# Perceiver layer on one core: key/value projection and cross attention in one loop over chunks, and the general path moved to the end

## The reference

```python
x = x + xattn(layernorm(x), ctx, ctx, ctx, ctx, ...)   # 16 heads of 32, 512 queries, keys: ctx twice
x = x + attn(layernorm(x), ...)                        # sequence axis of length 1: softmax is 1
x = x + ffn(layernorm(x), ...)                         # 8 experts, top 2, gelu, 512 -> 2048 -> 512
# xattn:
k = (jnp.einsum('bke,fe->bkf', k_full, wk) + bk).reshape(B, Lkv, H, D)
v = (jnp.einsum('bke,fe->bkf', v_full, wv) + bv).reshape(B, Lkv, H, D)
scores = jnp.einsum('bqhd,bkhd->bhqk', q, k) * scale
attn = jax.nn.softmax(scores, axis=-1)
ctx = jnp.einsum('bhqk,bkhd->bqhd', attn, v).reshape(B, Lq, E)
```

## Time and profile before

| | us |
|---|---|
| median of 3 runs (lowest, highest) | 1449.85 (1448.89, 1450.54) |
| the profiled execution | 1445.7 |
| its span, first to last instruction | 1443.9 |
| to the end of `project_queries` | 29.9 |
| projection of keys and values | 358.7 |
| end of that block, flag, skipped `find_maxima` | 8.0 |
| attention | 590.8 |
| cross output / self attention / routing | 27.1 / 35.4 / 29.1 |
| experts and end | 364.9 |

### The profile page before, as it was taken

How to read it: one execution, slowest core, us unless ns; L and a number is a source line. 1 busy time by engine, 2 the same in 40 slices (tenths; PEclk the granted TensorE clock), 3 DMA queues, 4 the chain that set the end, 5 groups by cost and what they waited for, 6 DMA issues and landing times. The chain is left out here.

```text
span 1443.9 us, 20528 instructions
## 1 busy us (share of the span) xinstructions
PE 1370.8 (95%) x7608; PEld 847.3 (59%) x7608; DVE 950.6 (66%) x819; ACT 772.9 (54%) x841; POOL 73.6 (5%) x71
## 2 busy tenths in 40 slices
PE   5999999999799999999999999998769999999995
PEld 4888888888643333333333333333557787887873
DVE  7444444444288888888888888887653566766662
ACT  4122221221088888888888888884222445555541
POOL 2000000000030000000000000000102010111110
PEclk9999999999999999999999999999955999999998
DMA  6854555556396555555555555520804666676641
GB/s 207 266 175 179 193 199 184 174 193 196 136 260 131 112 112 112 112 109 114 116 116 116 116 116 116 114 61 1 306 5 147 220 216 211 232 243 206 239 132 40
DMA packets 140900, 225.07 MB, mean 156 GB/s; under 512 B 8776, under 2 KB 41672, under 8 KB 140848
## 3 DMA queue, kind: packets, MB, share of 16 engines
q1 hardware_dynamic: 137520, 217.12, 51.7%
q0 software_dynamic: 3344, 7.47, 2.1%
HBM read 162.61 MB, written 59.85 MB: 154 GB/s over the span
## 5 line engine op out<-in xcount | busy, mean ns | idle before, releaser
L663 ACT ACTIVATE at_p<-at_s 128x1024 f32<-128x1024 f32 x512 | 496.9, 1023 | 90.7 <-PE at_s L616 90.6
L683 DVE TENSOR_TENSOR p_sum<-p_sum,at_p 128x2048 f32 (+1 forms) x208 | 476.7, 2292 | 58.1 <-ACT at_p L663 51.1
L616 PEld LDWEIGHTS at_s<-q_stack,at_k 97*128 97x128 f32 x1024 | 172.7, 189 | 248.5 <-ACT at_p L663 162.0
L616 PE MATMUL at_s<-q_stack,at_k 97*128 (+1 forms) x1024 | 311.4, 424 | 7.5 <-PEq L444 6.7
L629 PE MATMUL at_o<-at_p,at_v 128*32 128x512 f32 x2048 | 272.7, 605 | 0.1
L143 ACT ACTIVATE sc_c_hi<-sc_c 128x2048 fp32r<-128x2048 f32 x16 | 30.7, 1920 | 151.0 <-PE sc_vp L388 137.6
L413 ACT ACTIVATE sc_k_hi<-sc_kp,sc_bk 128x512 fp32r<-128x512 f32 x64 | 44.2, 691 | 125.4 <-PE sc_kp L381 125.4
L345 DVE SCALAR_TENSOR_TENSOR sc_k_lo<-sc_kp,sc_bk,sc_k_hi 128x512 fp32r<-128x512 f32 x64 | 47.8, 749 | 89.0 <-ACT sc_k_hi L413 89.0
L353 DVE TENSOR_TENSOR sc_v<-sc_vp,sc_bv 128x512 f32<-128x512 f32 x64 | 44.1, 689 | 88.8 <-PE sc_vp L388 88.8
L1268 ACT ACTIVATE se_h<-se_hp,se_b_cur 128x160 f32<-128x160 f32 x128 | 43.4, 391 | 105.4 <-PE se_hp L1203 105.4
L1255 ACT ACTIVATE se_wi_hi<-ei_wi 128x2048 fp32r<-128x2048 f32 x32 | 61.2, 1913 | 69.4 <-DVE se_b_cur L1314 69.1
(11 more groups left out here) (225 smaller groups left out, 1534.4 us busy)
## 6 DMA issues: line engine op xcount, KB each, us to landing
at_k<-k_hi_scratch SPq DMA_DIRECT2D x128, 256.0 KB, 4.8
ei_wi<-w_in SPq DMA_DIRECT2D x32, 1024.0 KB, 7.4
ei_wo<-w_out SPq DMA_DIRECT2D x32, 1024.0 KB, 5.5
sc_c<-ctx_t SPq DMA_DIRECT2D x16, 1024.0 KB, 7.9
k_hi_scratch<-sc_k_hi SPq DMA_DIRECT2D x16, 1024.0 KB, 4.0
k_lo_scratch<-sc_k_lo SPq DMA_DIRECT2D x16, 1024.0 KB, 6.1
at_k<-k_lo_scratch SPq DMA_DIRECT2D x64, 256.0 KB, 4.2
at_v<-v_scratch SPq DMA_DIRECT2D x64, 256.0 KB, 4.9
```

The lines of the kernel that those rows point to most:

```text
L616: last = nc.tensor.matmul(s[r][:, a * NQ:(a + 1) * NQ], k[c][:, j, t * P:(t + 1) * P], q_stack[:, bass.ds(it // PER_GROUP * (HG * NQ) + j ...
L663: nc.scalar.activation(p[t % PR][:, pair * 2 * NQ:(pair + 1) * 2 * NQ], s[u % SR][:, :], ACT.Exp, scale=SCALE).then_inc(p_ready[t % PR], 1)
L683: nc.vector.tensor_tensor(sums, sums, p[t % PR][:, :], ALU.add).then_inc(p_summed[t % PR], 1)
```

## The change

`stream_context`, the first `find_maxima` and `attend` are replaced by one block `attend_stream`. It projects the eight pieces of chunk 0 first; then, for every chunk, 16 steps (4 head groups by 4 key tiles) are worked in eight doubles of two steps, and one of the eight pieces of the next chunk is projected in each double (the last key group of a chunk in its own first double). Keys `k_hi`, `k_lo` (one buffer) and values (two) stay in SBUF; nothing goes to DRAM. Scores are no longer one product over 97 stacked rows: for each part the four heads of a group are four products over their own 32 rows, at row positions 0, 32, 64, 96, into four PSUM banks. All probabilities are summed by VectorE; `BY_PE` and `total_acc` go. Bank `o` now ends after 4 tiles. The value bias moves to the output: values carry no bias, and `cross_output` adds bv x Wo to the output bias. No bound is computed beforehand; `cross_output` looks at the logarithms of the totals (`good`), `route` joins that with the length flag to `again`. `any_path` holds the whole layer once more, in its general form (with maxima, any expert length), as eight stages in one block behind the output; each engine loads `again` once and guards each stage with it. Other edits: the late weights are loaded when the last projection is done; `turn_tokens` does its four large transposes and then its four small ones.

```diff
+def attend_stream(nc, ctx, c_dram, o_acc, p_sum, a, late, late_dram):
...
+    SR, PR = 3, 4
+    STEPS = NG * KT
+    DOUBLES = STEPS // 2
+    PAIRS = NCH // 2
+    k_hi, k_lo = (sb(f"k_{n}", [P, NG, CH], F32R) for n in ("hi", "lo"))
+    v = [sb(f"v{b}", [P, KT, E]) for b in range(2)]
+    p = [sb(f"p{r}", [P, HG * NQ]) for r in range(PR)]
+    s = [ctx.enter_context(nc.psum_tensor(f"as_s{r}", [P, 2 * NQ], F32)) for r in range(SR)]
+    o = ctx.enter_context(nc.psum_tensor("as_o", [P, NQ], F32))
+    proj = ctx.enter_context(nc.psum_tensor("as_proj", [P, CH], F32))
...
+    OUTPUTS = [("v", 0), ("k", 0), ("v", 1), ("k", 1), ("v", 2), ("k", 2), ("v", 3), ("k", 3)]
+    first_banks = [proj[:, :], o[:, :]] + [s[r][:, h * NQ:(h + 1) * NQ] for r in range(SR) for h in range(2)]
...
+            with sp.Fori(1, NCH) as m:
+                sp.wait_ge(c_lo_ready, ET * m)
+                sp.dma_start(c[:, :, :], c_dram.rearrange("(t p) n -> p t n", p=P)[:, :, bass.ds(m * CH, CH)]).then_inc(c_loaded, 16)
+            sp.wait_ge(k_done, NG * NCH)
+            for to, src in zip(late, late_dram):
...
+                for part, (lhs, rhs) in enumerate(products):
+                    for d in range(ET):
+                        if kind == "v":
+                            left, right = lhs[b][:, d, i * P:(i + 1) * P], rhs[:, d, E:2 * E]
+                        else:
+                            left, right = lhs[:, d, i * P:(i + 1) * P], rhs[b][:, d, :]
+                        last = nc.tensor.matmul(bank, left, right, start=(part == 0 and d == 0),
+                                                stop=(part == 2 and d == ET - 1))
+                last.then_inc(v_done if kind == "v" else k_done, 1)
+            def scores(i, b, step):
+                n, g, t = 2 * i + b, step // KT, step % KT
+                if t == 0:
+                    pe.wait_ge(k_lo_ready, NG * n + g + 1)
+                if isinstance(n, int) and n == 0 and step < 2:
+                    pe.wait_ge(k_lo_ready, NG - 1 + step)
+                    pe.wait_ge(v_ready, KT - 1 + step)
+                for pair in range(2):
+                    u = (b * STEPS + step) * 2 + pair
+                    if u >= SR:
+                        w = u - SR
+                        pe.wait_ge(p_ready[w // 2 % PR], exped(2 * i, w // 2, w % 2))
+                    else:
+                        w = s_last[u % SR]
+                        wait_reuse(pe, p_ready[w // 2 % PR], exped(2 * i - 2, w // 2, w % 2))
+                for part, (keys, queries) in enumerate(((k_hi, q_hi), (k_lo, q_hi), (k_hi, q_lo))):
+                    for j in range(HG):
+                        rows, r = slice(j * D, (j + 1) * D), ((b * STEPS + step) * 2 + j // 2) % SR
+                        last = nc.tensor.matmul(s[r][:, j % 2 * NQ:(j % 2 + 1) * NQ], keys[rows, g, t * P:(t + 1) * P],
+                                                queries[rows, g, :], start=(part == 0), stop=(part == 2))
+                        if part == 2 and j % 2 == 1:
+                            last.then_inc(s_ready[r], 1)
+            def outputs(n, b, step):
+                g, t = step // KT, step % KT
+                if t == 0:
+                    wait_reuse(pe, o_added, NG * n + g)
...
+                pe.wait_ge(p_ready[step % PR], exped(n, step, 1))
+                for j in range(HG):
+                    feats = slice(g * P + j * D, g * P + (j + 1) * D)
+                    last = nc.tensor.matmul(o[j * D:(j + 1) * D, :], v[b][:, t, feats], p[step % PR][:, j * NQ:(j + 1) * NQ],
+                                            start=(t == 0), stop=(t == KT - 1))
+                last.then_inc(p_used[step % PR], 1)
...
+                        scores(i, b, 2 * j)
+                        if j == 0 and not begins:
+                            project(n, b, *OUTPUTS[-1], proj[:, :], False)
+                        elif j > 0 and not ends:
+                            project(n + 1, 1 - b, *OUTPUTS[j - 1], proj[:, :], False)
+                        scores(i, b, 2 * j + 1)
+                        for step in (2 * j - 2, 2 * j - 1):
+                            if step >= 0:
+                                outputs(n, b, step)
+                            elif not begins:
+                                outputs(n - 1, 1 - b, step + STEPS)
+            for (kind, i), bank in zip(OUTPUTS, first_banks):
+                project(0, 0, kind, i, bank, True)
+            rolled(pe, PAIRS, pair)
...
+            def keep(m, b, kind, i, bank):
+                if kind == "v":
+                    if i == 0:
+                        wait_reuse(act, o_done, NG * (m - 1))
+                    act.wait_ge(v_done, KT * m + i + 1)
+                    nc.scalar.activation(v[b][:, i, :], bank, ACT.Copy).then_inc(v_ready, 1)
+                else:
+                    act.wait_ge(k_done, NG * m + i + 1)
+                    nc.scalar.activation(k_hi[:, i, :], bank, ACT.Identity, bias=bk[:, i:i + 1]).then_inc(k_hi_ready, 1)
...
+                        exps(i, b, 2 * j)
+                        if j == 0 and not begins:
+                            keep(n, b, *OUTPUTS[-1], proj[:, :])
+                        elif j > 0 and not ends:
+                            keep(n + 1, 1 - b, *OUTPUTS[j - 1], proj[:, :])
+                        if 2 <= j < 2 + ET and not last:
+                            split(n + 2, b, j - 2)
+                        exps(i, b, 2 * j + 1)
...
+            for (kind, i), bank in zip(OUTPUTS, first_banks):
+                keep(0, 0, kind, i, bank)
+            for d in range(ET):
+                split(1, 1, d)
...
+            def add_outputs(n, g):
+                dve.wait_ge(o_done, NG * n + g + 1)
+                if isinstance(n, int) and n == 0:
+                    nc.vector.tensor_copy(o_acc[:, g, :], o[:, :]).then_inc(o_added, 1)
+                else:
+                    nc.vector.tensor_tensor(o_acc[:, g, :], o_acc[:, g, :], o[:, :], ALU.add).then_inc(o_added, 1)
...
+                        add_probabilities(n, 2 * j)
+                        if j == 0 and not begins:
+                            keep_low(n, OUTPUTS[-1][1], proj[:, :])
+                        elif j > 0 and not ends and OUTPUTS[j - 1][0] == "k":
+                            keep_low(n + 1, OUTPUTS[j - 1][1], proj[:, :])
+                        if j % 2 == 1 and j > 1:
+                            add_outputs(n, (j - 3) // 2)
+                        elif j == 1 and not begins:
+                            add_outputs(n - 1, NG - 1)
+                        if 2 <= j < 2 + ET and not last:
+                            split(n + 2, b, j - 2)
+                        add_probabilities(n, 2 * j + 1)
...
@@ cross_output @@
+            pe.wait_ge(widened, NG + 1)
+            for g in range(NG):
+                last = nc.tensor.matmul(out[0][:, :], bv_wide[:, g, :], wo[:, g, :], start=(g == 0), stop=(g == NG - 1))
+            last.then_inc(bias_done, 1)
+            pe.wait_ge(bias_added, 1)
...
+            dve.wait_ge(bias_done, 1)
+            nc.vector.tensor_tensor(bo_all[:, :], bo[:, :], out[0][:, :], ALU.add).then_inc(bias_added, 1)
@@ route @@
+                last = nc.tensor.matmul(ranks[:, (QT + 1) * NX:(QT + 1) * NX + 1], every[:, :], good[:, :], start=True, stop=True)
@@ class General @@
+    def guarded(self, eng, name):
+        if name not in self.flags:
+            self.flags[name] = eng.value_load(self.flag[:, :], min_val=0, max_val=1)
+        with eng.If(self.flags[name] > 0):
...
+            self.meet(eng, 2 * self.stage - 1)
+            if name in self.programs:
+                self.programs[name](eng)
+            self.meet(eng, 2 * self.stage)
```

More of the change, by code:

```diff
@@ L21 @@
+import math
 from contextlib import ExitStack
@@ L319, in _ @@
-            for j in range(HG):
-                rows = slice(j * D, (j + 1) * D)
-                for part, src in enumerate((q_hi, q_hi, q_lo)):
-                    dst = q_stack[part * D:(part + 1) * D, :].bitcast(F32).rearrange("d (g j q) -> d g j q", j=HG, q=NQ)
-                    sp.dma_start(dst[:, :, j, :], src[rows, :, :].bitcast(F32)).then_inc(a.stacked, 16)
-            rolled(sp, PAIRS, pair)
-            sp.wait_ge(a.stacked, 16 * 3 * HG)
-            sp.wait_ge(stored[0], STORES * PAIRS)
@@ L699, in cross_output @@
-def cross_output(nc, ctx, wo, bo, o_acc, p_sum, total_acc, x_sb):
-    sb = lambda n, s, d=F32: ctx.enter_context(nc.sbuf_tensor(n, s, d))
-    sem = lambda n: ctx.enter_context(nc.semaphore(n))
+                    begins, ends = isinstance(n, int) and n == 0, last and b == 1
+                    for j in range(DOUBLES):
+                        add_probabilities(n, 2 * j)
[10 more added lines that the diff above has]
+                        add_probabilities(n, 2 * j + 1)
@@ new lines, in _, with cross_output @@
+            dve.wait_ge(a.biases, 16 * (1 + NG))
+            for (kind, i), bank in zip(OUTPUTS, first_banks):
+                if kind == "k":
```

(35 more changed lines are left out.)

1204 lines of the change are left out of this document (651 added, 553 removed).

## The result

The changed kernel takes 1509.71 us (median, 1506.93 to 1511.72) against 1449.37 us for the kernel before: a ratio of 1.0414 (95% interval 1.0391 to 1.0437), 60 us slower. The prediction, 1459 us with a range from 1420 to 1590, had the sign and the range, but its value lies 51 us too low.

A forecast was written before the change was run, and what follows sets the result against it. TensorE, busy in 95% of the span, was taken as the bound; -6 + 1.5 + 0.6 - 3.5 + 16.5 = +9.1 on 1445.7 us gave 1454.8, put at 1459 us for the runs' median, range 1420 to 1590.

The forecast's parts named there:

- Scores, 0.87 us: In the attention, twelve score products in four row groups run as three rounds, 0.87 us in all.
- Rivals 1 to 3: Score products: row groups' loads in line (15%, 1582 us); rounds wait for own loads (6%, 1530); no overlap (5%, 1865).
- rival 3: Row groups do not overlap in the scores: 2.9 us a score, both doubles 10.5, kernel 1865 us; chance 5%.
- Doubles 6.50 and 8.05: Inner loop: even doubles take 6.50 us, odd ones 8.05 because the outputs wait for VectorE's `add_outputs`; a chunk 58.2.
- the 1.3 to 1.7 us of my signs: Expected in the new profile: in every odd double the first output product starts 1.3 to 1.7 us late.
- Loop's return: At the chunk loop's branch back: 6 x 0.31 = 1.9 us, possibly a full code fetch, 6 x 3.7 = 22.
- First and last chunk: First eight projections and first chunk 78.4 us; last chunk, without projections, 53.4 + 3 us.
- The end, +16.5: Behind the output: eight guarded stages skipped 19 us, minus the old skip 3.9, plus 1.4; range +5 to +28.
- `cross_output` +0.7, `route` +0.4, experts -3.2: Stages after the attention: predicted `cross_output` +1.5 us, `route` +0.6, the experts' `turn_tokens` transposes -3.5.
- over 90% busy in the loop: Expected in the new profile: VectorE, which now makes all 256 sums, over 90% busy in the loop.
- Rival 5: The flag is set and the general path at the end runs: about 1400 us more; chance 1%.
- rival 4: In odd doubles the wait for `o_added` does not bind: every double 6.5 us, -96, kernel 1363 us; chance 9%.

The follow-up runs named there:

- experiment 11: The kernel with the three edits, all twelve score products of a step taking keys and queries from rows 0 to 31; 2095.92 us.
- experiment 2: The changed kernel with VectorE adding the outputs ahead of the first probability sum in odd doubles; 1419.26 us, ratio 0.9791.
- experiment 1: The changed kernel with the 16 chunks as straight code, no loop, on TensorE, ScalarE and VectorE; 1476.29 us, ratio 1.0194.
- experiments 3 and 6: Each against the changed kernel: 3 puts the eight general-path stages under one guard per engine, 1487.12 us; 6 leaves the general path out, 1481.28 us.
- the three edits: The changed kernel with straight code for the chunks, VectorE's output addition first and one guard around the general path, together; 1364.53 us, ratio 0.9415.
- 10: The kernel with the three edits, its twelve score products ordered head by head, all three of one head before the next; 1370.51 us.

## Why the prediction was off, step by step

- **Scores, 0.87 us: right** (0.90 to the next mode). Rivals 1 to 3 (loads in line, rounds that wait for their loads, no overlap) are refuted by the trace, and experiment 11 shows what rival 3 would have looked like.
- **Doubles 6.50 and 8.05: right in mechanism and size** (6.64 and 7.86). The even one lacked 0.14 us, 0.10 of it in the first step of the projection behind the scores, which takes 0.33 instead of 0.23. In the odd double shown the wait is 1.14 us, not 1.55: TensorE is ready 0.18 later than I had it, and the outputs start 0.23 earlier. The wait thus falls short of the 1.3 to 1.7 us of my signs. A pair is 14.5 against 14.55, a chunk 57.9 to 58.0 against 58.2. I had named the wait as 6.2 us of each chunk and did not ask on whose order of work it hung; experiment 2 shows that moving one addition removes it.
- **Loop's return: the failed step.** "The loop's return cost the attention 0.31 us [...]: 6 x 0.31 = 1.9; it could be a full code fetch as below, 6 x 3.7 = 22." Both halves of the lower value failed. The row at 468.02 isn't the return, and the body had grown from 216 products a pass to 832, which no longer stay loaded. It measured 5 x 7.5 = 37 us. Even my upper end was low, since it counted one load of 3.7 us: behind the branch comes a second stretch of 2.9 us without a step, so that 5.0 us pass without products, and then the clock is at the lower level for some 6 us. This one term is 35 of the 51 us. "A gap of microseconds at the loop's return" stood among my signs of being wrong, and it was there.
- **First and last chunk: +5 and +6 us.** Both are stretches in which TensorE pauses and then works at the lower level for a part; my sum had every duration at full clock. In the last chunk the odd doubles take 9.2 to 9.6 us, not 8.05, with longer waits for `o_acc` besides. In experiment 1, whose last chunk took 66.5 us, the same effect ate 3.7 of its gain.
- **The end, +16.5: too low by 8.6.** The mechanism was right (eight skips by TensorE alone, nothing hides them; experiments 3 and 6). The long ones cost 4.4 to 5.0 us, not 3.75 (18.7 instead of 15.0). Of the short ones, which I had put at 1 each, two cost 0.22 and 0.35 and two 3.41 and 3.36: the eight prices fall into 0.2 to 0.4 and 3.4 to 5.0 us, with nothing between. The flag's load and the barrier hold the other 1.5 us.
- **`self_attention`, 0 predicted, +2.8.** The same instructions; the clock rose to the full level at 1069, 18 us into the stage, instead of at 1025, 11 us into it. The other kernels, unchanged there, have 35.3 to 38.3 us for this stage. It belongs to no edit.
- **`cross_output` +0.7, `route` +0.4, experts -3.2: right.** The transposes gained more than I said (0.90 instead of 1.69 us, 5.5 in all), and part went into waits for the split output weights (2.6 us instead of 1.2); the rest of the difference I did not trace.
- **VectorE, "over 90% busy in the loop": wrong.** It is busy in 76% of two ordinary chunks (88.2 of 115.9 us from 148.3 to 264.2), so the cause of the wait was its order and not its load.
- **Rival 5**, the run of the general path, did not come; **rival 4**, that the wait does not bind, is refuted. That its 1363 us is what the three edits gave (1364.5) is chance: they got there by other means. (Its -96 us is 62 odd doubles at 1.55 us; 64 would be -99.)

## What to carry to other kernels

Before a loop's price is taken from an old trace, compare the bodies' sizes: TensorE's branch back took 0.2 us up to 640 products with their loads and 3.3 to 3.8 at 832, where it left 5.0 us without a product and another 2.5 us at the lower clock. The instruction packets in the DMA view tell which of the two a loop is. And look up the branch itself before calling a long product the return. Where an engine waits for another's small operation, look at what that engine does just before it: here 0.7 us of work stood behind a 2.3 us sum for no reason, and a reordering gave 90 us, more than anything else. While such a wait is there, removing work from the waiting engine may gain nothing: two thirds fewer score and projection products left the chunk as long as it was.

## What the hardware showed that I had not expected

- TensorE took products out of the order of the code where row groups differ, unless the tool that built the kernel did (see 10): twelve products in the order 0,0,0,1,1,1,2,2,2,3,3,3 take 0.92 us up to the next mode, as in the order 0,1,2,3 (0.90), and 2.94 when all stand in one group. The Trainium skill's page TensorE: Matmul & The Clock Gate (Part 3) says that matmuls start and end strictly in program order; the trace of 10 differs from that, and that of 11, with one row group, doesn't.
- Skipping a guarded block cost TensorE either 3.4 to 5.0 us or 0.2 to 0.4; of the four stages that I had counted as short, two fell on each side. The other engines paid less: ScalarE had passed all eight guards by 1480, VectorE by 1488, TensorE by 1505.
- TensorE's granted clock fell again and again while the profile shows the engine busy without a pause: 0.87 on the mean in experiment 11.
- A loop whose body no longer stays loaded shows in the DMA view: 36 instruction packets in four passes with 832 products, none with 640.
